# Gate folded into both projections of a fused attention and mixture-of-experts kernel, with the outer products and the block steps dealt out anew

## The reference

```python
x = x + attention(layernorm(x))   # 16 heads of 8; Q K^T masked causally, no softmax, times V; wo, bias
xm = layernorm(x)
probs = softmax(xm @ Wg)          # 8 experts
topk_p, topk_i = top_k(probs, 2)
for e in range(8):                # for the tokens that picked e
    y_e = relu(xm @ W1[e] + b1[e]) @ W2[e] + b2[e]     # 128 -> 256 -> 128
x = x + sum over the two picks of topk_p * y_e
```

## Time and profile before

| | us |
|---|---|
| median of 3 runs | 308.99 (307.54 to 309.55) |
| the profiled execution | 308.35 |
| its span, first to last instruction | 306.6 |
| TensorE busy, mean granted clock | 244.9, 0.916 |
| VectorE, ScalarE, GpSimd busy | 195.5, 174.1, 179.1 |

### The profile page before, as it was taken

How to read it: one execution, slowest core, us unless ns; L and a number is a source line. 1 busy time by engine, 2 the same in 40 slices (tenths; PEclk the granted TensorE clock), 3 DMA queues, 4 the chain that set the end, 5 groups by cost and what they waited for, 6 DMA issues and landing times.

```text
span 306.6 us, 6357 instructions
## 1 busy us (share of the span) xinstructions
PE 244.9 (80%) x1392; PEld 176.5 (58%) x1392; DVE 195.5 (64%) x584; ACT 174.1 (57%) x701; POOL 179.1 (58%) x175
## 2 busy tenths in 40 slices
PE   0589999999999999987779976969399999896000
PEld 0234566666666666655557865857388778774000
DVE  5938999889998989999652456323143343342184
ACT  3243358888888888777678743445155556552000
POOL 3255492205868686876361777777777676676100
PEclk9999999999999999999566998899689999999655
DMA  7940000000111110111160222234443333211499
GB/s 208 310 145 0 1 2 0 0 4 17 37 37 35 38 36 28 43 36 55 34 169 17 62 74 66 70 84 127 132 116 103 92 89 87 68 47 36 155 356 310
DMA packets 32400, 25.50 MB, mean 83 GB/s; under 512 B 4305, under 2 KB 30169, under 8 KB 32364
## 3 DMA queue, kind: packets, MB, share of 16 engines
q1 hardware_dynamic: 23808, 14.52, 17.6%
q0 software_dynamic: 4320, 8.47, 8.4%
q10 hardware_dynamic: 4236, 2.10, 2.3%
HBM read 13.92 MB, written 11.61 MB: 83 GB/s over the span
## 4 chain that ended last, share of the span: by engine, by line
PE 53%; issue 13%; DVE 10%; DMA 9%; POOL 5%; ACT 4%; SPq 3%; ACTq 1%; POOLq 0%; DVEq 0%
PE ps L870 17%; PE ps L840 8%; PE ps L967 6%; PE ps L956 6%; POOL returned L402 4%; DMA back<-returned 3%; PE ps L879 2%; DMA returned<-y_sb,xt 2%; PE ps L892 2%; PE ps L842 2%; SPq L321 2%; DVE back L623 2%; POOL dispatched L374 2%; DVE o_sb L636 2%; PE ps L861 2%
## 5 line engine op out<-in xcount | busy, mean ns | idle before, releaser
L402 POOL DMA_INDIRECT returned<-y_sb,xt x71 | 70.4, 991 | 34.2 <-issue 20.9
L374 POOL DMA_INDIRECT dispatched<-rows,slot x64 | 64.3, 1005 | 37.8 <-ACT rows L473 21.5
L793 DVE TENSOR_SCALAR y_sb<-ps,xt 128x128 f32<-128x128 f32 x71 | 24.9, 350 | 73.4 <-PE ps L968 72.4
L870 PE MATMUL ps<-back,causal 128*128 128x512 f32 x128 | 62.8, 614 | 0.4 <-DVE back L614 0.4
L967 PE MATMUL ps<-w_sb,hT 128*128 x284 | 52.1, 309 | 6.4 <-DVE y_sb L793 4.8
L956 PE MATMUL ps<-xT,w_of 128*128 128x128 f32 x284 | 50.0, 302 | 2.7 <-ACT hT L546 1.9
L538 ACT ACTIVATE xT<-ps 128x128 f32<-128x128 f32 x71 | 19.6, 276 | 55.6 <-PE ps L949 54.4
L967 PEld LDWEIGHTS ps<-w_sb,hT 128*128 128x128 f32 x284 | 40.1, 204 | 19.0 <-issue 18.8
L358 POOL TENSOR_TENSOR back<-qkv 128x1024 f32<-128x1024 f32 x16 | 31.3, 1955 | 31.4 <-ACT qkv L494 31.1
L546 ACT ACTIVATE hT<-ps,b_col 128x128 f32<-128x128 f32 x142 | 43.9, 364 | 1.7 <-PE ps L956 1.4
L956 PEld LDWEIGHTS ps<-xT,w_of 128*128 128x128 f32 x284 | 40.0, 204 | 5.0 <-issue 4.1
(11 more groups left out here) (142 smaller groups left out, 415.9 us busy)
## 6 DMA issues: line engine op xcount, KB each, us to landing
xt<-dispatched SPq DMA_DIRECT2D x71, 65.0 KB, 2.0
back<-returned SPq DMA_DIRECT2D x8, 512.0 KB, 7.6
x_sb<-x SPq DMA_DIRECT2D x8, 256.0 KB, 5.0
out<-x_sb ACTq DMA_DIRECT2D x8, 256.0 KB, 6.6
returned<-y_sb,xt POOLq DMA_INDIRECT x71, 2.3
w_sb<-w SPq DMA_DIRECT2D x1, 1024.0 KB, 5.9
w_sb<-w SPq DMA_DIRECT2D x2, 512.0 KB, 7.2
dispatched<-rows,slot POOLq DMA_INDIRECT x64, 2.4
```

The source lines that it names most:

```text
L374: pool.indirect_dma_start(out=dispatched[:, :], out_offset=bass.IndirectOffsetOnAxis(ap=slot[:, g * K + k:g * K + k + 1], axis=0), in_=row ...
L402: pool.indirect_dma_start(out=returned[:, :], out_offset=bass.IndirectOffsetOnAxis(ap=xt[:, n % G, D:D + 1].bitcast(I32), axis=0), in_=y_s ...
L793: dve.tensor_scalar(y_sb[:, n % G, :], ps_y, xt[:, n % G, D + 1:D + 2], None, ALU.mult).then_inc(y_done, 1)
L870: mm = pe.matmul(ps_run[g % 2][:, u, :], causal[:, :], outer[:, g % OUTER_RING, 512 * u:512 * (u + 1)], start=True, stop=True)
```

## The change

- **The gate moves into the projections.** The logits are layernorm(x2) @ Wg, where x2 = x + attention. With the columns of Wg centred (their mean subtracted), they are rstd2 * (x2 @ centred Wg). So 8 columns more in the first projection give the normalized x times the centred gate, which ScalarE scales back by the standard deviation (`std1`) and puts beside x (x_sb is now 136 wide); 8 columns more in the output projection, wo times the centred gate, give the attention's part. `add_residual` adds both. VectorE multiplies by rstd2 before the softmax (`lg`). `transpose2`, `xn2T_out` and `gate` are gone. The centred weights and the second projection's 8 columns and bias are worked out in the first slots (`gate_weights`, `gate_bias_split`).
- **Outer products.** VectorE does those of tiles 13, 16, 19, 22, 25, 28 and 31; GpSimd the other 25. GpSimd's splitting of the last bias is spread over steps 9 to 11.
- **Block steps.** STEPS is 3. The steps that read registers (k from -3 to -1) are in the slot before; the first count and table come three and two slots earlier. GpSimd sends two blocks in each of the steps 39 to 43, one from 44 to 47. The counts and the second table come after later block steps. The lag of the dispatches (16) stays.

```diff
+    DISPATCH = 16
+    FIRST_COUNT = N
+    BLOCKS_FROM = N + 4
+    XE = D + E
...
-    STEPS = 2
+    STEPS = 3
...
+        def on_vector(g):
+            return g >= 12 and g % 3 == 1
+
+        def outers(g, vector):
+            return sum(on_vector(i) == vector for i in range(g + 1))
...
             load_x(0).then_inc(x_in[0], 16)
-            sp.dma_start(wqkv_sb[:, :], w_qkv).then_inc(w_qkv_in, 16)
+            sp.dma_start(wg_sb[:, :], w_gate).then_inc(w_g_in, 16)
+            sp.dma_start(wqkv_sb[:, 0:3 * D], w_qkv).then_inc(w_qkv_in, 16)
             load_x(1).then_inc(x_in[1], 16)
-            sp.dma_start(wo_sb[:, :], w_o).then_inc(w_o_in, 16)
+            sp.dma_start(wo_sb[:, 0:D], w_o).then_inc(w_o_in, 16)
+            sp.dma_start(bo_col[:, :], b_o.rearrange("(d one) -> d one", one=1)).then_inc(bo_in, 16)
...
+                batch_after = T * (EARLY + 1) - 1 + DISPATCH
+                more = 2 if batch_after <= s <= batch_after + T else 1 if s > batch_after else 0
...
+                act.activation(std1[:, own.start:own.stop], log1[:, own.start:own.stop], ACT.Exp, scale=0.5).then_inc(std_done, 1)
...
             def qkv_out(g):
                 old = g - QKV_RING
                 wait(act, qkv_mm, g + 1)
-                wait(act, outer_pool, old // 2 + 1)
-                wait(act, outer_dve, (old + 1) // 2)
+                wait(act, outer_pool, outers(old, False))
+                wait(act, outer_dve, outers(old, True))
                 wait(act, prod_done, old + 1)
                 wait(act, kv_done, states(old - old % T + T - 1))
+                wait(act, std_done, 1 + (g >= AHEAD[1].start) + (g >= AHEAD[2].start))
+                act.activation(x_sb[:, g, D:XE], ps_xg, ACT.Identity, scale=std1[:, g:g + 1]).then_inc(xg_done, 1)
                 act.activation(qkv[:, g % QKV_RING, :], ps_qkv, ACT.Identity).then_inc(qkv_done, 1)
...
-            def xn2T_out(g):
-                wait(act, T2_done, g + 1)
-                wait(act, lg_mm, g + 1 - RING)
-                act.activation(xn2T[:, g % RING, :], ps_T2, ACT.Identity).then_inc(xn2T_done, 1)
+            def gate_weights(g):
+                if g == 2:
+                    act.wait_ge(woT_mm, 1)
+                    act.activation(woT[:, :], ps_woT, ACT.Identity).then_inc(woT_done, 1)
+                elif g == 4:
+                    act.wait_ge(gate_mm, 1)
+                    act.activation(wo_sb[:, D:XE], ps_wo_gate, ACT.Identity).then_inc(gate_done, 1)
+                    act.activation(gate_bias[:, :], ps_bo_gate, ACT.Identity).then_inc(gate_done, 1)
...
-            k = -3
+            k = 0
             for s in range(-2, N + 13):
                 for lag, stage in tile_stages:
                     if 0 <= s - lag < N:
                         stage(s - lag)
-                if s >= N + 4:
+                if s == BLOCKS_FROM - 1:
+                    for before in (-3, -2, -1):
+                        block_step(block_stages, before)
+                if s >= BLOCKS_FROM:
                     for _ in range(STEPS):
...
             def add_residual(g):
                 wait(dve, att_mm, g + 1)
-                dve.tensor_tensor(tile(g), ps_att, tile(g), ALU.add).then_inc(x2_done, 1)
+                wait(dve, xg_done, g + 1)
+                dve.tensor_tensor(x_sb[:, g, :], ps_att, x_sb[:, g, :], ALU.add).then_inc(x2_done, 1)
 
             def outer_product(g):
-                if g % 2 == 0:
+                if not on_vector(g):
...
             def softmax_start(g):
                 if g % T < T - 1:
                     return
-                wait(dve, lg_mm, g + 1)
-                dve.tensor_reduce(gmax[:, :], ps_lg, AX_X, ALU.max).then_inc(gmax_done, 1)
+                b = g // T
+                wait(dve, rstd2_done, g + 1)
+                wait(dve, x2_done, g + 1)
+                dve.tensor_tensor(lg[:, :, :], x_sb[:, b * T:(b + 1) * T, D:XE],
+                                  norm2[:, b * T:(b + 1) * T, 0].unsqueeze(2).to_broadcast([P, T, E]), ALU.mult).then_inc(lg_done, 1)
+                wait(dve, lg_done, b + 1)
+                dve.tensor_reduce(gmax[:, :], lg[:, :, :], AX_X, ALU.max).then_inc(gmax_done, 1)
                 wait(dve, gmax_done, batches(g))
-                dve.tensor_tensor(shifted[:, :, :], ps_lg, over_e(gmax), ALU.subtract).then_inc(shift_done, 1)
+                dve.tensor_tensor(shifted[:, :, :], lg[:, :, :], over_e(gmax), ALU.subtract).then_inc(shift_done, 1)
...
+            dve.wait_ge(w_g_in, 16)
+            dve.wait_ge(average_mm, 1)
+            dve.tensor_tensor(wqkv_sb[:, 3 * D:3 * D + E], wg_sb[:, :], ps_average, ALU.subtract).then_inc(centred, 1)
...
-            k = -3
+                           (9, places), (2, state_out), (-2, outer_product), (-2, gate_bias_split)]
+            k = 0
             for s in range(-2, N + 9):
                 for lag, stage in tile_stages:
                     if 0 <= s - lag < N:
                         stage(s - lag)
-                    if s == N and stage is add_residual:
+                    if s == FIRST_COUNT - 3 and stage is add_residual:
                         count_first()
-                if s == N:
+                if s == FIRST_COUNT - 2:
                     first_table()
                 elif s == N + 3:
                     left_by_first()
-                if s > N:
+                if s == BLOCKS_FROM - 4:
+                    for before in (-3, -2, -1):
+                        block_step(block_stages, before)
+                if s > BLOCKS_FROM - 4:
                     for _ in range(STEPS):
                         block_step(block_stages, k)
                         k += 1
-            for _ in range(2 * STEPS):
+            for _ in range(4):
...
             def project(g):
                 wait(pe, xnT_done, g + 1)
                 wait(pe, qkv_done, g)
-                wait(pe, shift_done, batches(g - 12))
-                pe.matmul(ps_qkv, xnT[:, g % RING, :], wqkv_sb[:, :], start=True, stop=False)
+                wait(pe, xg_done, g)
+                if g == 0:
+                    pe.wait_ge(centred, 1)
+                pe.matmul(ps_qkvg, xnT[:, g % RING, :], wqkv_sb[:, :], start=True, stop=False)
                 wait(pe, bias_done, 4)
                 pe.matmul(ps_qkv, ones[:, :], bias_parts[:, 0:3 * D], start=False, stop=True).then_inc(qkv_mm, 1)
...
             def project_out(g):
                 wait(pe, oT_done, g + 1)
                 wait(pe, x2_done, g)
-                if g == N - T:
+                if g == FIRST_COUNT - 7:
                     pe.wait_ge(cnt_read, 1)
                 if g == 0:
+                    pe.wait_ge(gate_bias_done, 3)
+                pe.matmul(ps_att, oT[:, g % RING, :], wo_sb[:, :], start=True, stop=False)
+                pe.matmul(ps_att, ones[:, :], bias_parts[:, 3 * D:4 * D + E], start=False, stop=True).then_inc(att_mm, 1)
+
+            def gate_weights(g):
+                if g == 1:
                     pe.wait_ge(w_o_in, 16)
-                pe.matmul(ps_att, oT[:, g % RING, :], wo_sb[:, :], start=True, stop=False)
-                pe.matmul(ps_att, ones[:, :], bias_parts[:, 3 * D:4 * D], start=False, stop=True).then_inc(att_mm, 1)
-
-            def transpose2(g):
-                wait(pe, rows_done, g + 1)
-                wait(pe, oT_done, g + 4, N)
-                wait(pe, xn2T_done, g)
-                pe.transpose(ps_T2, rows[:, g, 0, 0:D], ident[:, :]).then_inc(T2_done, 1)
-
-            def gate(g):
-                wait(pe, xn2T_done, g + 1)
-                wait(pe, qkv_done, g + 12, N)
-                wait(pe, shift_done, batches(g - 1))
-                if g == 0:
-                    pe.wait_ge(w_g_in, 16)
-                pe.matmul(ps_lg[:, g % T, :], xn2T[:, g % RING, :], wg_sb[:, :], start=True, stop=True).then_inc(lg_mm, 1)
+                    pe.transpose(ps_woT, wo_sb[:, 0:D], ident[:, :]).then_inc(woT_mm, 1)
+                elif g == 3:
+                    pe.wait_ge(woT_done, 1)
+                    pe.wait_ge(bo_done, 1)
+                    pe.matmul(ps_wo_gate, woT[:, :], wqkv_sb[:, 3 * D:3 * D + E], start=True, stop=True)
+                    pe.matmul(ps_bo_gate, bo_wide[:, :], wqkv_sb[:, 3 * D:3 * D + E], start=True, stop=True).then_inc(gate_mm, 1)
...
-            tile_stages = [(3, running_sums), (11, gate), (5, q_transposed), (7, o_transposed), (5, sum_state), (-1, project),
-                           (-2, transpose1), (10, transpose2), (7, project_out), (12, rank)]
-            k = -3
+            tile_stages = [(3, running_sums), (5, q_transposed), (7, o_transposed), (5, sum_state), (-1, project),
+                           (-2, transpose1), (7, project_out), (12, rank), (0, gate_weights)]
+            k = 0
             for s in range(-2, N + 12):
-                if s == N + 3:
-                    pe.wait_ge(x2_done, N - T)
+                if s == FIRST_COUNT:
+                    pe.wait_ge(x2_done, FIRST_COUNT - 7)
```

(7 more changed lines are left out.)

99 lines of the change are left out of this document (67 added, 32 removed).

## The result

The changed kernel takes **324.35 us** (median of 4 runs, 323.75 to 324.72) against 308.65 for the kernel before: ratio 1.051, interval 1.047 to 1.055. A second series gave 1.049 (1.043 to 1.056). Its profiled execution spans 322.5 us at a mean clock of 0.888. The forecast of 308.3, and its range up to 312.8, were wrong.

What follows compares the result with a forecast made beforehand. Nearly full engines bound the steady stage, tile 24's dispatch the rest. Steady -5.9 and early +1.3 gave -4.6; late slots left that dispatch at 170.1 against 170.57, so 308.35 - 0.5, plus 0.64, stated as 308.3 us; range 303.3 to 312.8.

Steps and rivals of the forecast that it cites:

- C: GpSimd's dispatch of tile 24, on which both late limits were said to hang; 170.57 us before, forecast 170.1.
- nothing but C moves: Late half: if only the dispatch of tile 24 shifts, the whole time shifts with it one for one.
- (b): Rival: three-step slots at the lower clock, 21.8 us for slots 37 to 39, hold `chosen` back; 312.4 us, chance 0.11.
- (c): Rival: the steady slot gets no shorter, as GpSimd's groups or the shared port set the pace; 312.5 us, chance 0.07.
- Early stage: First slots: ScalarE's copy and `std1`, extra TensorE work and loads add +1.3 us (+0.3 to +2).
- a rule against the change: Instructions reading two SBUF tensors may be held by GpSimd products on the shared port; 16 VectorE softmax instructions, 8 us.
- VectorE has no idle time there, so this only reorders it: Earlier first count and table: VectorE's work merely changes order; `add_residual(28)` near 146.2, slot 37 at 148.8.
- I count three quarters of 7.9: -5.9: Steady stage: the removed gate and transpose save 7.9 us if TensorE alone counted; -5.9 taken, bounds -7.9 and -2.
- The bound of -2: Steady stage: the smallest saving allowed for the removed gate and transpose, 2 us against the 5.9 taken.
- The estimate of 8 us: Steady stage: 16 `lg` and `shifted` instructions, GpSimd product running half the time, 1.0 us each: 8 us late.
- the 18.9 us: Late slots 37 to 39 with three block steps each: 6.9 + 6.2 + 5.8 = 18.9 us on ScalarE.
- 170.1 against 170.57: Dispatch of tile 24: 148.8 + 18.9 + 2.4 = 170.1 us forecast, against 170.57 in the kernel before.

Runs made afterwards that it cites:

- e4: The changed kernel with outer products dealt as before, odd tiles on VectorE and even ones on GpSimd: ratio 1.035.
- e9: The kernel before plus the gate through the projections, bias split from PSUM and seven outer products on VectorE, old schedule: 305.1 us, ratio 0.986.
- e11: The kernel before plus only the gate through the projections, bias split from PSUM, outer products in turn: 306.5 us, ratio 0.991.
- e10: The kernel before with only the change's schedule (early count and table, pre-steps, three block steps begun at 0, sends): 320.3 us, ratio 1.037.
- e7: The changed kernel with bias split from PSUM, count, first table and register reads late, two block steps and sends as before: 310.0 us, ratio 1.004.

## Why the prediction was wrong

**What bounds the kernel: right.** C to send 15, C to the last send and "nothing but C moves" held wherever the loads landed early: 112.1 to 113.5 us from C to the last send in nine traces, from the fastest kernel to the changed one. Block 32's transpose came at 235.90, 49.4 after C, as forecast. `chosen` took over from the sends as what releases C, as forecast. Of the rivals (b) and (c) had the right side and no size: (b) needed 21.8 us for slots 37 to 39, which took 19.5.

Two slips of arithmetic stand in the prediction, and neither is the reason: 307.9 + 0.64 is 308.5, not 308.3, and the shift of rival (c) is 1.3 - 0.7 = +0.6, not -0.6, which puts its C at 175.3 and its time near 313.7, above the stated range.

**The steps between.** C was forecast at 170.1 and came at 186.46, 16.4 us later. The forecast had running sum 31 at 133.75 (138.35 - 4.6); it came at 148.75, 15.0 later. From there to slot 37 I had 15.05 and it took 14.65; slot 37 to C was 21.3 and took 23.1. So **15.0 of the 16.4 us arose before running sum 31**, and three terms make it up:

- *Early stage, sum "+1.3 (+0.3 to +2)": +7.05.* The step that failed most. I listed the early stage's instructions on TensorE and ScalarE and its loads, and never priced `gate_bias_split` on VectorE against the GpSimd products beside it: its six instructions have no term in the sum. Nor has the reverse side of "nine outer products leave VectorE": they go to GpSimd, whose products then run back to back beside the split (`e4`). From running sum 0 to 4 the change took 11.38 us, before 12.43, so the rest of that term was too dear. Then `gate_bias_split` came: running sum 8 at 55.17 instead of 48.12 in `e9`. I had given the lengthening of the earlier trace rows as a rule against the change, and applied it only to `lg` and `shifted`.
- *"VectorE has no idle time there, so this only reorders it": +5.2.* From running sum 28 to 31 the changed kernel took 16.22 us, `e9` 11.01. The step looked at VectorE's order and not at TensorE's: the count became a wait ahead of a running sum. By time the early count costs 310.6 - 305.1 = 5.5 us.
- *"I count three quarters of 7.9: -5.9": +2.75.* `e9` leads by 1.86 us at running sum 31, not 4.6. Over running sums 8 to 28 the change took 77.4 us, before 79.4: 0.10 a slot instead of 0.25. The bound of -2 was the right value. (This is net of the early stage, which without the split came out 1.2 us better than my +1.3: `e9` is level with the kernel before at running sum 8, 48.12 and 47.98.)

7.05 + 5.2 + 2.75 = 15.0.

**Rival (c) and the rule.** `lg` was held, but only twice in eight (1.13 and 1.62 us in the changed kernel instead of 0.18), and `shifted` never: 2.4 us instead of 8. The estimate of 8 us took a GpSimd product as running for half of the steady stage; by the prediction's own numbers (10 products of 1.96 us in four groups of 14.6 us) it is a third. Here is the `lg` in slot 19 of `e9`, VectorE, ScalarE and GpSimd:

```profile
77.03 1.62 DVE L690 TENSOR_TENSOR lg<-x_sb,norm 128x32 f32<-128x32 f32 x1
...
79.13 0.23 ACT L538 ACTIVATE expd<-shifted 128x32 f32<-128x32 f32 x1 [1.41 <-DVE shifted L695]
...
76.63 1.96 POOL L386 TENSOR_TENSOR back<-qkv 128x1024 f32<-128x1024 f32 x1
```

It made that slot 4.97 us long (before 3.96). The remaining loss of the steady stage was put to VectorE, which with one outer product in three is 96% busy over it; with one in two (`e11`) it is 98% busy and the stretch takes 62.3 us instead of 62.8. Of `e9`'s stretch about 1.0 us is the held `lg`, which `e11` does not have (two slots there take 9.18 us in `e9` and 8.23 in `e11`); apart from that `e11` is 0.5 us longer, with some 2.5 us more work on VectorE. So VectorE's busy share over the stretch does not set the pace. What is seen is where the loss lies, in the two slots of each four with top two and places; that VectorE's burst there is the cause was argued and not tested alone.

**Three block steps: the 18.9 us were right, "170.1 against 170.57" was not.** I compared slots 37 to 39 with a release by sends that came 5.3 us after `chosen`, and took the stretch for free up to there. But GpSimd's first sends depend on the same slots, and with two steps begun at -3 they come early too: in `e9` C is 167.78. Beginning the steps at 0 costs 310.0 - 305.1 = 4.9 us (two series; by their ratios 5.5), the third step 3.7 (4.4 in the second series).

**The sum.** From `e9` to the changed kernel: 7.7 + 5.5 + 4.9 + 3.7 = 21.8 us against 324.3 - 305.1 = 19.2 measured. The pieces come from three chips; by ratios they add up to 0.068 against 0.063, a difference that the intervals (0.007 either way for the changed kernel) do not resolve. If they overlap, a likely part is the table, which comes early with the early count and then shortens block 0's wait, but no run separates that. The schedule's three parts, 14.1 us, gave 11.1 in `e10`.

## What to carry to other kernels

When an instruction is added to VectorE, read what GpSimd does at that moment before its size: eight columns cost 1.9 us beside a GpSimd product and 0.16 us with the source in PSUM. When a step is moved earlier, list what stands behind it in the order of every engine that executes or waits for a part of it, and check there whether its input exists already; what was "only reordered" on one engine made another wait and cost 5.5 us in all. And a change of several parts should be run part by part, and in pairs where two parts meet: here a gain of 4 us was hidden under 19 us that the way it was built in cost, and the largest loss came from two parts together.

## What the runs showed of the hardware

While a GpSimd product on 128x1024 elements ran, VectorE's SBUF-to-SBUF casts of 8 columns and its instructions on two SBUF tensors of 8 or 32 columns lasted until it ended (1.13 to 1.88 us instead of 0.17 to 0.18). Instructions with a PSUM source did not, nor did a reduction or a reciprocal. In `e9` the first cast of the split, now out of PSUM, lies wholly inside the very product that held it in the changed kernel:

```profile
30.72 2.13 POOL L413 TENSOR_TENSOR b_bc<-b_bc,b_high 128x1024 f32<-128x1024 f32 x1
...
31.06 0.16 DVE L771 CAST gate_high<-ps 128x8 bf16<-128x8 f32 x1
```

In `e7` these three lie wholly inside a GpSimd product:

```profile
81.23 1.97 POOL L386 TENSOR_TENSOR back<-qkv 128x1024 f32<-128x1024 f32 x1
...
82.49 0.22 DVE L717 TENSOR_TENSOR pick<-top_i,ps 128x64 f32<-128x64 uint32 x1 [0.68 <-PE ps L935]
82.62 0.17 DVE L721 RECIPROCAL grec<-gsum 128x4 f32<-128x4 f32 x1
82.74 0.22 DVE L724 TENSOR_REDUCE picked<-pick 128x32 bf16<-128x64 f32 x1
```

The Trainium skill (SBUF — State Buffer, "SBUF: two separate sides") calls the pair of ports that VectorE and GpSimd share an exclusive lock, taken for the whole instruction by whichever starts first, when VectorE runs in a two-port mode or has two SBUF inputs; by that rule the trace agrees for the instructions on two SBUF tensors, and for the casts if they ran in a two-port mode, which no trace shows.

Both long waits of TensorE cost more than their length. After 4.74 and 3.28 us without work the granted clock was 0.60 and 0.50 over the next running sum, which took 3.22 and 3.78 us; at 1.00, running sum 28 took 1.93.
